# Moving layer 2's keys to the heads of layer 1's two stages, and layer 3's values into the return stage of layer 2's routed rows

## The reference

```python
x = x + _L0_ffn_ref(_layernorm(x), ...)                 # 8 experts of 1024, all computed
x = x + _L1_xattn_ref(_layernorm(x), ctx_1024, W, b)    # x1 @ W1.T + mean(ctx @ W2.T) + b
x = x + _L1_ffn_ref(_layernorm(x), ...)                 # 64 small experts and 2 shared ones
# layer 2's attention
Q = q_in @ Wq.T + bq
K = k_in @ Wk.T + bk                                    # k_in and v_in are ctx_1024
V = v_in @ Wv.T + bv
w = softmax(Q K^T * scale + beta terms of fside)
x = x + w @ V
x = x + _L2_ffn_ref(_layernorm(x), ...)                 # shared part, and top 2 of 8 experts
# layer 3's attention, and beside it an MLP; a vote on row 0 of each batch picks one of the two
e0 = softmax(q k^T * scale) (ctx_1024 Wv) Wo
e1 = gelu(x @ W1 + b1) @ W2 + b2
x = x + where(vote == 0, e0, e1)
x = x + _L3_ffn_ref(_layernorm(x), rhs)                 # int8 matmul
```

## Time and profile before

| | |
|---|---|
| median of the runs | 1528.09 us (1527.57 to 1533.8) |
| profiled execution | 1529.01 us, of which the span of instructions is 1527.0 us |
| mean granted TensorE clock | 0.946 |
| PE busy | 1397.2 us (92%), 8362 matmuls |
| PEld busy | 1122.4 us (74%) |
| DVE busy | 896.7 us (59%) |
| ACT busy | 693.7 us (45%) |
| POOL busy | 353.0 us (23%) |

### The profile page before, as it was taken

How to read it: one execution, slowest core, us unless ns; L and a number is a source line. 1 busy time by engine, 2 the same in 40 slices (tenths; PEclk the granted TensorE clock), 3 DMA queues, 4 the chain that set the end, 5 groups by cost and what they waited for, 6 DMA issues and landing times. The chain is left out here.

```text
span 1527.0 us, 24679 instructions
## 1 busy us (share of the span) xinstructions
PE 1397.2 (92%) x8362; PEld 1122.4 (74%) x8362; DVE 896.7 (59%) x1704; ACT 693.7 (45%) x1134; POOL 353.0 (23%) x365
## 2 busy tenths in 40 slices
PE   5799999799999999999999699999989798993994
PEld 4544444588898888889888587888877687882893
DVE  6778887744555555555555843444466657544456
ACT  5366667343443443344343165555543354452431
POOL 2102224311221222122121122333310056331000
PEclk8889999889999999999999799999999989996996
DMA  6802220211111111111110114555422134323000
GB/s 226 254 15 51 53 64 16 62 41 51 41 41 62 41 41 57 46 41 42 61 41 7 49 43 117 145 143 142 124 81 83 41 118 142 94 91 107 1 1 27
DMA packets 63799, 110.83 MB, mean 73 GB/s; under 512 B 10331, under 2 KB 39517, under 8 KB 62845
## 3 DMA queue, kind: packets, MB, share of 16 engines
q1 hardware_dynamic: 61869, 104.93, 23.3%
q0 software_dynamic: 1872, 5.13, 0.9%
HBM read 90.91 MB, written 18.97 MB: 72 GB/s over the span
## 5 line engine op out<-in xcount | busy, mean ns | idle before, releaser
L1217 DVE TENSOR_TENSOR hidden_l<-silu_l,up_l 128x512 f32<-128x512 f32 x128 | 88.1, 688 | 219.9 <-ACT silu_l L1157 219.9
L1157 ACT ACTIVATE silu_l<-gate_l 128x512 f32<-128x512 f32 x128 | 76.6, 599 | 308.5 <-PE up_l L75 308.5
L851 DVE TENSOR_REDUCE maxima<-a_scores 128x1 f32<-128x512 f32 x256 | 164.6, 686 | 41.4 <-PE a_scores L790 40.0
L73 PE MATMUL out_l<-dn_hi_l,h_hi_l 128*128 128x256 f32 x576 | 164.0, 285 | 7.6 <-DVE h_lo_l L2472 7.6
L75 PE MATMUL out_l<-dn_hi_l,h_lo_l 128*128 128x256 f32 x576 | 163.6, 284 | 0.0
L74 PE MATMUL out_l<-dn_lo_l,h_hi_l 128*128 128x256 f32 x576 | 163.6, 284 | 0.0
L818 ACT ACTIVATE probs<-b_scores 128x1024 f32<-128x1024 f32 x128 | 131.1, 1024 | 67.0 <-PE b_scores L747 64.9
L1189 POOL TENSOR_TENSOR gu_lo_l<-gu_raw_l,gu_hi_l 128x1024 fp32r<-128x1024 f32 x31 | 74.4, 2399 | 298.8 <-ACT gu_hi_l L1149 298.8
L1241 DVE SCALAR_TENSOR_TENSOR x_sb<-out_l,cw,x_sb 128x256 f32<-128x256 f32 x256 | 109.0, 478 | 22.4 <-PE out_l L75 18.1
L73 PEld LDWEIGHTS out_l<-dn_hi_l,h_hi_l 128*128 128x128 f32 x576 | 110.9, 192 | 11.0 <-ACT h_hi_l L2365 6.2
L73 PE MATMUL gate_l<-xnT_hi_n,gu_hi_l 128*128 128x512 f32 x288 | 115.2, 400 | 1.7 <-ACT xnT_hi_n L220 1.2
(11 more groups left out here) (451 smaller groups left out, 3382.6 us busy)
## 6 DMA issues: line engine op xcount, KB each, us to landing
gu_raw_l<-w_units SPq DMA_DIRECT2D x32, 512.0 KB, 3.9
spread_l<-cw_rows SPq DMA_DIRECT2D x64, 256.0 KB, 3.8
dn_raw_l<-w_units SPq DMA_DIRECT2D x32, 256.0 KB, 2.6
k_stack<-k_stacks SPq DMA_DIRECT2D x8, 768.0 KB, 5.7
staged_l<-w_experts SPq DMA_DIRECT2D x24, 256.0 KB, 2.7
up_raw_l<-w SPq DMA_DIRECT2D x40, 128.5 KB, 3.4
dn_raw_l<-w SPq DMA_DIRECT2D x40, 128.0 KB, 2.0
phi_a<-fside SPq DMA_DIRECT2D x8, 512.0 KB, 3.2
```

The costliest lines, as they stand in the source:

```text
L73: pe.matmul(out, lhs[0], rhs[0], start=start, stop=False, skip_group_check=True)
L851: dve.tensor_reduce(maxima[k // 16][:, i // 2, i % 2:i % 2 + 1], a_scores[:, k % 2, :], X, ALU.max).then_inc(a_read, 1)
L1157: act.activation(silu[:, q % 2, :], gate[:, q % 2, :], ACT.Silu).then_inc(silu_done, 1)
L1217: dve.tensor_tensor(hidden[:, q % 2, :], silu[:, q % 2, :], up[:, q % 2, :], ALU.mult).then_inc(hidden_done, 1)
```

## The change

Layer 2's weights are loaded at the start of layer 0's feed-forward phase and split by POOL at its end. Layer 2's 8 key tiles leave `l2_project_phase`: three of them (`KEYS_EARLY`) are computed at the head of `l1_shift_phase`, in the PSUM banks of `out_s`, and five at the head of `l1_experts_phase`, in those of `front_l`. The projection keeps 12 tiles.

In `l2_sparse_phase` the weights and halves of the shared part, and the normalised rows, now lie in the SBUF that holds layer 3's values later; SP loads Wv and Wo of layer 3 before the fourth block of routed rows, and POOL splits them ahead of its first indirect DMA. Its wait for all of these DMAs to land goes; SP has it at the head of the return phase instead. The return phase gets the product Wv·Wo and the 8 value tiles; VectorE writes four low halves first, then one after each addition. `l3_front_phase` has neither any more, loads one pair of weights instead of two, and its hidden tiles come right after the one weight tile left. Memory for keys and values is allocated earlier.

```diff
+KEY_TILES, KEYS_EARLY = KC * CT // 512, 3
...
+                sp.dma_start(g.wqkv2.raw[:, :, :, :], d["wqkv2"]).then_inc(g.wqkv2.loaded, 16)
...
+                split_l2_weights(pool, g)
...
+def key_tile(pe, g, n, bank):
+    fc, t = n % KC, n // KC * 512
+    f = slice(fc * P, (fc + 1) * P)
+    for k in range(KC):
+        last = mm3(pe, bank, (g.wqkv2.hi[:, 1, k, f], g.wqkv2.lo[:, 1, k, f]),
+                   (g.ctxT_hi[:, k, t:t + 512], g.ctxT_lo[:, k, t:t + 512]), k == 0, k == KC - 1)
+    last.then_inc(g.key_tile_done, 1)
+def key_high(act, g, n, bank):
+    fc, t = n % KC, n // KC * 512
+    act.wait_ge(g.key_tile_done, n + 1)
+    act.activation(g.kT_hi[:, fc, t:t + 512], bank, ACT.Identity, bias=g.bias_cols[:, BK2, fc:fc + 1]).then_inc(g.key_hi_done, 1)
+def key_low(dve, g, n, bank):
+    fc, t = n % KC, n // KC * 512
+    dve.wait_ge(g.key_hi_done, n + 1)
+    dve.scalar_tensor_tensor(g.kT_lo[:, fc, t:t + 512], bank, g.bias_cols[:, BK2, fc:fc + 1], f32(g.kT_hi[:, fc, t:t + 512]),
+                             ALU.add, ALU.subtract).then_inc(g.key_lo_done, 1)
...
+                for n in range(KEYS_EARLY):
+                    key_high(act, g, n, key_banks[:, n, :])
                 norm.high(act, 0)
                 norm.high(act, 1)
...
                 norm.apply(dve, 1)
+                key_low(dve, g, 0, key_banks[:, 0, :])
                 norm.low(dve, 0)
                 norm.low(dve, 1)
+                for n in range(1, KEYS_EARLY):
+                    key_low(dve, g, n, key_banks[:, n, :])
...
+                pe.wait_ge(g.wqkv2.split_done, 2)
+                for n in range(KEYS_EARLY):
+                    key_tile(pe, g, n, key_banks[:, n, :])
                 norm.turn(pe, 0)
-                pe.wait_ge(lo_done, 1)
-                pe.wait_ge(mean_lo_done, 1)
+                pe.wait_ge(lo_done, 2)
...
                 norm.turn(pe, 1)
                 for m in range(TC // 2):
                     norm.wait_half(pe, m // 2)
+                    if m < KEYS_EARLY:
+                        pe.wait_ge(g.key_lo_done, m + 1)
                     if m == LAST:
-                        pe.wait_ge(shift_done, 1)
+                        pe.wait_ge(mean_shift_done, 2)
...
-                sp.dma_start(g.wqkv2.raw[:, :, :, :], d["wqkv2"]).then_inc(g.wqkv2.loaded, 16)
...
                             if first:
+                                pe.wait_ge(g.key_lo_done, KEYS_EARLY + 3 + q)
                                 norm.wait_half(pe, q)
...
+                for n in range(KEYS_EARLY, KEY_TILES):
+                    if n >= KEYS_EARLY + 4:
+                        pe.wait_ge(g.key_lo_done, n - 3)
+                    key_tile(pe, g, n, key_bank(n))
                 norm.on_tensor(pe)
-                periods(pe, period, {0: router.take_logits, 5: router.turn_weights, 7: add_biases})
+                def take_logits(pe):
+                    pe.wait_ge(g.key_lo_done, KEY_TILES)
+                    router.take_logits(pe)
+                periods(pe, period, {0: take_logits, 5: router.turn_weights, 7: add_biases})
...
                 split_up(0, 0, 1)
+                for n in range(KEYS_EARLY, KEY_TILES):
+                    key_high(act, g, n, key_bank(n))
                 norm.high(act, 0)
...
-                split_l2_weights(pool, g)
...
+                norm.apply(dve, 1)
+                for n in range(KEYS_EARLY, KEY_TILES - 1):
+                    key_low(dve, g, n, key_bank(n))
+                norm.low(dve, 0)
+                norm.low(dve, 1)
+                key_low(dve, g, KEY_TILES - 1, key_bank(KEY_TILES - 1))
...
-        tiles = [(K, fc, t) for t in range(0, CT, 512) for fc in range(KC)]
-        tiles += [(V, None, m) for m in range(CT // P // 2)]
+        tiles = [(V, None, m) for m in range(CT // P // 2)]
         tiles += [(Q, fc, t) for t in range(0, T, 512) for fc in range(KC)]
...
+                sp.wait_ge(h_hi_done, 2 * N)
+                sp.wait_ge(h_lo_done, 2 * N)
+                sp.dma_start(pair_raw, d["wqkvo3"][:, 2:4, :, :]).then_inc(pair_loaded, 16)
...
+                pool.wait_ge(pair_loaded, 16)
+                pool.wait_ge(gu_done, 2 * N)
+                pool.tensor_copy(g.pair_hi, pair_raw).then_inc(pair_split, 1)
+                pool.wait_ge(pair_split, 1)
+                pool.tensor_tensor(g.pair_lo, pair_raw, f32(g.pair_hi), ALU.subtract).then_inc(pair_split, 1)
+                pool.wait_ge(pair_split, 2)
...
-                for i in range(OUTS):
-                    pool.wait_ge(scattered[i], 16 * len(range(i, NB2, OUTS)))
...
+                for done, count in g.scattered2:
+                    sp.wait_ge(done, count)
...
+            @block.tensor
+            def _(pe):
+                for c in range(KC):
+                    f = slice(c * P, (c + 1) * P)
+                    for k in range(KC):
+                        last = mm3(pe, product[:, c, :], (g.pair_hi[:, 0, k, f], g.pair_lo[:, 0, k, f]),
+                                   (g.pair_hi[:, 1, k, :], g.pair_lo[:, 1, k, :]), c == 0 and k == 0, k == KC - 1)
+                last.then_inc(product_done, 1)
+                pe.wait_ge(w_hi_done, 1)
+                pe.wait_ge(w_lo_done, 1)
+                for m in range(TILES):
+                    if m >= 4:
+                        pe.wait_ge(v_lo_done, m - 3)
+                    for j in range(2):
+                        t = slice((2 * m + j) * P, (2 * m + j + 1) * P)
+                        for k in range(KC):
+                            last = mm3(pe, acc[:, m % 4, j * D:(j + 1) * D], (g.ctxT_hi[:, k, t], g.ctxT_lo[:, k, t]),
+                                       (w_hi[:, k, :], w_lo[:, k, :]), j == 0 and k == 0, k == KC - 1)
+                    last.then_inc(values_done, 1)
+            @block.scalar
+            def _(act):
+                act.wait_ge(product_done, 1)
+                act.activation(w_hi[:, :, :], product[:, :, :], ACT.Copy).then_inc(w_hi_done, 1)
+                for m in range(TILES):
+                    act.wait_ge(values_done, m + 1)
+                    act.activation(v_of(g.v_hi, m), acc[:, m % 4, :], ACT.Copy).then_inc(v_hi_done, 1)
...
+                def low(m):
+                    dve.wait_ge(v_hi_done, m + 1)
+                    dve.tensor_tensor(v_of(g.v_lo, m), acc[:, m % 4, :], f32(v_of(g.v_hi, m)), ALU.subtract).then_inc(v_lo_done, 1)
...
-                sum_parts(0)
-                for i in range(PIECE):
-                    add_parts(i)
-                    if i + 1 < PIECE:
-                        sum_parts(i + 1)
+                def stats(i):
                     dve.wait_ge(added, i + 1)
                     take_stats(dve, g, (2 * i, 2 * i + 1))
+                dve.wait_ge(w_hi_done, 1)
+                dve.tensor_tensor(w_lo[:, :, :], product[:, :, :], f32(w_hi[:, :, :]), ALU.subtract).then_inc(w_lo_done, 1)
+                EARLY = TILES - PIECE
+                for m in range(EARLY):
+                    low(m)
+                for i in range(PIECE):
+                    sum_parts(i)
+                    add_parts(i)
+                    low(EARLY + i)
+                    stats(i)
...
-        tiles = [("weight", 1), ("value", 0), ("value", 1), ("weight", 0)] + [("value", m) for m in range(2, CT // P // 2)]
+        tiles = [("weight", 0)]
...
-                split_pair(1)
-                norm.high(act, 0)
-                split_pair(0)
-                high(0)
-                norm.high(act, 1)
+                split_pair()
                 act.wait_ge(mlp_loaded, 32)
                 act.activation(mlp_hi[:, :, :, :], mlp_raw[:, :, :, :], ACT.Copy).then_inc(mlp_hi_done, 1)
                 act.activation(wg_hi[:, :, :], wg_raw[:, :, :], ACT.Copy).then_inc(mlp_hi_done, 1)
+                norm.high(act, 0)
+                norm.high(act, 1)
+                high(0)
                 for n in range(1, NH):
```

More of the change, by code:

```diff
@@ L1762, in _ @@
                     else:
[L1763 removed]
+                        src = g.xnT_hi, g.xnT_lo
                         f = slice(fc * P, (fc + 1) * P)
@@ L2616, in halves @@
             if kind == "weight":
-                return w_hi[:, what, :, :], w_lo[:, what, :, :]
-            if kind == "value":
-                return g.v_hi[:, 2 * what:2 * what + 2, :], g.v_lo[:, 2 * what:2 * what + 2, :]
+                return w_hi[:, :, :], w_lo[:, :, :]
             fc, h = what
@@ L2685, in tile @@
                             pe.wait_ge(mlp_lo_done, 2)
-                        weights, which = ((mlp_hi, mlp_lo), 0) if kind == "hidden" else ((w_hi, w_lo), 0)
-                        last = product(bank, both(*weights, which, None, slice(fc * P, (fc + 1) * P)), both(g.xnT_hi, g.xnT_lo, None, slice(h * 512, (h + 1) * 512)))
+                        if kind == "query" and fc == 0:
+                            pe.wait_ge(tile_read, at["weight", 0] + 1)
+                        cols = slice(fc * P, (fc + 1) * P)
```

(2 more changed lines are left out.)

145 lines of the change are left out of this document (77 added, 68 removed).

## The result

The changed kernel takes 1522.73 us (median of 11 runs, 1519.76 to 1530.09) against 1529.07 for the kernel before (11 runs): ratio 0.9959, interval 0.9945 to 0.9974, so 4 to 8 us faster, with 6.3 in the middle. The forecast was -9.9. The measured 1522.73 lies inside the wide range (1512.5 to 1524.5), above the forecast's own range (1515.5 to 1521.5) and above the 1520.5 that counted as faster by 0.5%, which had been given a chance of 0.70.

A forecast was written before the change was run, and what follows sets the result against it. TensorE, busy 92% of the span, was read as the bound, so moved tiles needed its idle time. A +0.6, B +4.9, C -10.3, R +9.2, F -14.3 sum to -9.9: 1518.2 us, own range 1515.5 to 1521.5, wide 1512.5 to 1524.5.

The forecast's parts named there:

- C: Layer 2's projection: 48 matmuls of 8 key tiles go; -10.3 us, between -9.5 and -11.
- A: Layer 1's shift stage: three key tiles added, mostly covered by the normalisation; +0.6 us, bounds +0.3 and +1.9.
- B: Head of layer 1's experts: five key tiles make the first experts' tile start later; +4.9 us, bounds +4.1 and +6.9.
- first rival: TensorE stays at 1.2 GHz after its new starts in A, B and R: +12.1, sum +2.2, 1530.3 us; chance 0.06.
- The rest: Layer 0's weight load and POOL split, and the routed rows: 0 us; at most +3.5 for the split, +/-0.5 routed rows.
- R: Return stage: product and value tiles added, loads starting 1.0 us sooner; +9.2 us, bounds +5.8 and +10.5.
- the sign that was to prove the forecast wrong: A granted clock of 0.5 in the return stage's value tiles would show the forecast wrong.
- second rival: POOL's DMA wait held the return stage: 5.3 us gap goes but for 1, sum -13.3, 1514.8 us; chance 0.17.
- The third: Rival: moved tiles cost nearly as much in their new places; sum -3.6, 1524.5 us; chance 0.17.
- F: Layer 3's front stage: eight value tiles, one weight tile and a wait go; -14.3 us, between -13.5 and -15.1.

The follow-up runs named there:

- e1: The changed kernel with only layer 2's keys moved; routed rows, return and front stage as in the kernel before; ratio 0.9994 against the kernel before.
- e3: The changed kernel once more, unaltered, for a second profile; median 1523.58 us, ratio 0.9947 against the kernel before.
- e9: As e4, but the eighth key tile moves from the experts' head into the middle of the router's logits; 1514.68 us, ratio 0.9898.
- e2: The kernel before with only layer 3's values moved (routed rows, return and front stage of the changed kernel); ratio 0.9948 against the kernel before.
- e4: The changed kernel with VectorE's return-stage order altered: two low halves in each of four rounds, not four ahead of the first sum; 1518.64 us, ratio 0.9909.

## Why the prediction was right in its range and off in its sum

**C** (-10.3): -10.0 in the first profile, -10.7 in e1 and e3. Right.

**A** (+0.6): +0.9 to +1.3. The mechanism was right: the shift starts 0.9 to 1.3 us later in the stage than before, behind two more low halves. The end of the range, +1.9, was not reached; the clock rose 3.5 us after the start.

**B** (+4.9): the mechanism of the head was right, and its size was +5.8 instead. The step that failed is "the stage that follows has no idle time to give back": true, but the stage could also take more. The first rival, a slow clock, had the right actor in the wrong place: it looked for the 1.2 GHz in the keys themselves, at the start; there the clock rose in 4.4 us. It fell 13.7 us after that rise, during the logits. With 3 to 4.4 us of that, B is +8.8 to +10.2, outside its bounds (+4.1 to +6.9), and the keys together are A + B + C = -1.0 to +1.5 before the attention is counted.

**The rest** (0): right for layer 0, for POOL's split and for the routed rows. Wrong for layer 2's attention: I took it as untouched because no line of it changes. With the projection 10 us shorter, TensorE enters it at the full clock, ends its first scores in 5.7 us instead of 7.3 and then waits for a load and the softmax; 3.9 to 5.2 us were lost there, with 10.2 to 13.7 us at 0.50 in that stage where it had been 6.8. The term of 0 for this stage is the second step that failed: the same stage could also have gained, for in e9, without any slow time, it takes 61.8 us in place of 64.4. e1's ratio of 0.9994, where its profile's stages A to attention add up to +2.9 and layer 3 gives some 4 back (its front 2.2, its attention 2.4), fits.

**R** (+9.2): 27.6 - 18.0 = +9.6, in e2 and e3 +9.4 and +7.8. Right, with rounds and order as forecast, but two errors nearly cancel: the start is 1.6 sooner instead of 1.0, and the stage is 11.2 longer instead of 10.2. In this profile the clock rose 8.5 us after TensorE's start; in e3 it rose 3.4 us after, and the stage is 1.8 shorter. That is the first rival in this one stage, at a price of 1 us to the first sum and not 5.8, and the sign that was to prove the forecast wrong, 0.50 in the value tiles, holds for their first 4 us there and not in e3. The second rival (a start 4.3 sooner) is out: it was 1.6. The third has the nearest sum (-3.6), but not by its terms: the rounds didn't grow, the hidden tiles of the front stage start 10.1 us in, as forecast (10 to 11), and B went beyond it. That the order on VectorE and not TensorE set the end was used in the sum but not seen as something to be had: e4 takes some of it, 1.7 to 3.5 us in the stage and about 5 by the medians.

**F** (-14.3): -14.4, in e2 and e3 -15.6 and -15.7. Right, rather more than less.

So the forecast of -9.9 was for B and the attention 8 to 10 us too good on one side, and 2 to 4 too bad on the other (F, and layer 3's attention, 1.1 to 2.6 shorter in the profiles, for which I have no cause shown). That the result still lies in the wide range is partly luck, since F, layer 3's attention and in e3 R came out better than forecast for reasons that the forecast didn't have. Measured: -6.3 here, and -7.4 at e3's chip (1530.98 to 1523.58).

## What to carry to other kernels

Work moved into an idle place is paid not only there: what follows is shifted too, and TensorE's clock answers to that, so compare the granted clock of the next stages, not only the moved tiles. A run of narrow matmuls counts as busy in a profile, but the clock can fall during it; with a few wide ones in its middle it stayed up in the one profile of each of the three kernels where that was tried, without a gain in the whole runs that stands clear of their spread. A load that is waited for at the head of a stage is worth a look in stages that the change doesn't touch, once they start sooner or faster. And where one engine serves two streams (here VectorE the value tiles and the additions), don't let it wait for the later stream first: going by what is ready first brought about 5 us on top of the 8 that the place of the values had brought (e4, e2), where the place of the keys had brought nothing (e1).
